# Weighting expert results on the way out of PSUM and adding them into memory with an accumulating scatter, in a decoder layer with a mixture of experts

## What is computed

```python
x = hidden_states.reshape(-1, 512)                       # 2048 tokens
topk_indices, topk_weights = router(x)                    # 2 of 16 experts for each token, weights sum to 1
combine = zeros(2048, 16).at[arange(2048)[:, None], topk_indices].add(topk_weights)
h1 = einsum('th,ehi->tei', x, w_up)                       # w_up (16, 512, 256)
a = relu(h1)**2 * combine[:, :, None]
routed = einsum('tei,eih->th', a, w_down)                 # w_down (16, 256, 512)
shared = relu(hidden_states @ shared_up)**2 @ shared_down
out = x_residual + routed + shared
```

## Time and profile before

| | |
|---|---|
| median of 3 runs | 1241.31 us (1241.05 to 1241.61) |
| profiled execution, its own time | 1238.74 us |
| its span in the trace | 1236.9 us |
| TensorE busy in the span | 1073.2 us (87%) |
| VectorE, ScalarE, GpSimd busy | 806.6, 668.3, 673.2 us |
| DMA | 94.74 MB, mean 77 GB/s |

### The profile page before, as it was taken

How to read it: one execution, slowest core, us unless ns; L and a number is a source line. 1 busy time by engine, 2 the same in 40 slices (tenths; PEclk the granted TensorE clock), 3 DMA queues, 4 the chain that set the end, 5 groups by cost and what they waited for, 6 DMA issues and landing times. The chain is left out here.

```text
span 1236.9 us, 18614 instructions
## 1 busy us (share of the span) xinstructions
PE 1073.2 (87%) x6368; PEld 642.0 (52%) x6368; DVE 806.6 (65%) x1195; ACT 668.3 (54%) x1438; POOL 673.2 (54%) x587
## 2 busy tenths in 40 slices
PE   7999838888888888888888899999999989999970
PEld 3444325555555555555555444444444457676740
DVE  5477779999999999999999476631760013333327
ACT  3566768889888888898888424202010012223220
POOL 1033369999999999999999630202041124444430
PEclk9999959999999999999999999999999999999995
DMA  6210001101111111111331212103027314333219
GB/s 204 87 36 19 18 18 35 35 28 35 35 36 32 30 35 36 36 33 63 95 102 45 90 48 103 69 34 116 20 79 244 102 44 128 127 128 129 77 49 385
DMA packets 51820, 94.74 MB, mean 77 GB/s; under 512 B 9806, under 2 KB 17998, under 8 KB 51728
## 3 DMA queue, kind: packets, MB, share of 16 engines
q1 hardware_dynamic: 44208, 72.82, 17.9%
q0 software_dynamic: 7520, 20.72, 5.4%
HBM read 74.51 MB, written 20.84 MB: 77 GB/s over the span
## 5 line engine op out<-in xcount | busy, mean ns | idle before, releaser
L604 POOL TENSOR_TENSOR w_all<-w_all 128x512 f32<-128x512 f32 x256 | 321.1, 1275 | 0.6 <-POOLq L96 0.3
L778 DVE TENSOR_TENSOR_SCAN w_all<-da,w_all 128x512 f32<-128x512 f32 x256 | 298.0, 1206 | 0.0
L712 ACT ACTIVATE da<-w_all,a_flat 128x512 f32<-128x512 f32 x256 | 179.6, 702 | 9.0 <-PEq L96 7.7
L683 PE MATMUL yb<-ident,w_all 128*128 128x128 f32 x1024 | 161.6, 281 | 7.5 <-DVE acc L786 7.5
L633 PE MATMUL sc<-w_all,attn 32*128 32x384 f32 (+3 forms) x512 | 105.0, 486 | 45.5 <-ACT w_all L720 22.8
L720 ACT ACTIVATE w_all<-sc,neg_max 128x128 f32<-128x128 f32 (+3 forms) x256 | 134.1, 539 | 16.5 <-DVE neg_max L770 15.5
L659 PE MATMUL ob<-w_all,v 128*32 128x128 f32 x1280 | 94.7, 277 | 52.8 <-ACT w_all L729 52.8
L683 PEld LDWEIGHTS yb<-ident,w_all 128*128 128x128 f32 x1024 | 113.5, 141 | 37.0 <-issue 30.6
L770 DVE TENSOR_REDUCE neg_max<-sc 128x2 f32<-128x256 f32 (+3 forms) x128 | 104.2, 814 | 34.2 <-PE sc L636 34.2
L1166 POOL TENSOR_TENSOR w_all<-w_all 128x512 f32<-128x512 f32 x24 | 29.4, 1226 | 165.0 <-ACT w_all L1337 165.0
L729 ACT ACTIVATE w_all<-tb 128x256 f32<-128x256 f32 (+2 forms) x192 | 102.8, 535 | 29.7 <-PE tb L648 29.7
(11 more groups left out here) (199 smaller groups left out, 1630.6 us busy)
## 6 DMA issues: line engine op xcount, KB each, us to landing
w_all<-b_scratch SPq DMA_DIRECT2D x64, 256.0 KB, 3.3
w_all<-in_w_up SPq DMA_DIRECT2D x16, 512.0 KB, 6.0
w_all<-in_w_down SPq DMA_DIRECT2D x16, 512.0 KB, 6.8
w_all<-sorted_y SPq DMA_DIRECT2D x16, 512.0 KB, 10.3
attn<-in_x SPq DMA_DIRECT2D x4, 1024.0 KB, 6.8
w_all<-in_x SPq DMA_DIRECT2D x16, 256.0 KB, 4.1
norms<-attn SPq DMA_DIRECT2D x4, 1024.0 KB, 4.3
out_dram<-acc SPq DMA_DIRECT2D x16, 256.0 KB, 8.9
```

What stands on the lines that cost most here:

```text
L604: pool.tensor_tensor(dbu[:, k, :], keep["du"][i // N][:, k * T:(k + 1) * T], b_all[i % 2][:, :], ALU.mult).then_inc(pool_dbu.sem, pool_dbu ...
L683: last = pe.transpose(yb[which][:, k * P:(k + 1) * P], state[i % 2][:, k, t * P:(t + 1) * P], ident[:, :])
L712: act.activation(da[unit % 2][:, :], keep["dt"][i // N][:, k * T:(k + 1) * T], ACT.Exp, scale=keep["a_flat"][:, unit % (N * KD):unit % (N ...
L778: dve.tensor_tensor_scan(state[i % 2][:, k, :], da[unit % 2][:, :], dbu[:, k, :], 0.0, ALU.mult, ALU.add).then_inc(dve_scan.sem, dve_scan. ...
```

## The change

The four things that it does:

1. The router also sorts the weights. Each weight, in float32, is cut into three bfloat16 parts (`high`, `mid`, `low`); three more planes are made from them, `collect` takes five planes at once (235 columns where 94 were), and `tokens` adds the three parts up to `slot_weight`, a weight for each slot.
2. ScalarE's copy of a tile's result out of PSUM multiplies by `slot_weight`.
3. The scatter adds: with `compute_op=ALU.add` it adds each row of `y` to the token's own row of `sorted_y`, in which `base` was stored before. A token has two pairs, in different tiles, so each scatter waits for the one before it to land. Padding is no longer dropped; it goes to 128 spare rows.
4. `acc` is stored to `sorted_y` in `close` (4 MB in 7 DMAs, `store_base`), and at the end 8 DMAs of 512 KB copy `sorted_y` to `out`, from memory to memory. The read back, the 32 instructions of VectorE and the 16 output DMAs are gone.

The scratch of the router moves with it (slot 15 of the weights is used, so expert 15 is loaded behind `s_routed`; `prob` and `tmp` lie in it).

```diff
 class Router:
...
-        self.prob = sb("prob", [P, TT, E])
+        self.prob = room[2][:, 0:TT * E].rearrange("p (t e) -> p t e", e=E)
...
-            last = pe.matmul(out[:, 0:2 * SLOT_TILES], self.in_row[:, n, :], self.planes[:, n, :, :].rearrange("p w i -> p (w i)"),
+            last = pe.matmul(out[:, 0:PLANES * SLOT_TILES], self.in_row[:, n, :], self.planes[:, n, :, :].rearrange("p w i -> p (w i)"),
                              start=(n == 0), stop=(n == 2 * B * NT - 1))
...
         for w, token in enumerate((self.token_hi, self.token_lo)):
             self.link(dve, dve.tensor_tensor(self.planes[:, :, w, :], self.in_tile[:, :, :], over(token[:, :], NI), ALU.mult))
+        weight = self.r["weight_all"][:, :]
+        high, mid, low = [x[:, :] for x in self.part_bf]
+        left, rest = [x[:, :] for x in self.part]
+        self.link(dve, dve.tensor_copy(high, weight))
+        self.link(dve, dve.tensor_tensor(left, weight, high, ALU.subtract))
+        self.link(dve, dve.tensor_copy(mid, left))
+        self.link(dve, dve.tensor_tensor(rest, left, mid, ALU.subtract))
+        self.link(dve, dve.tensor_copy(low, rest))
+        for w, part in enumerate((high, mid, low)):
+            self.link(dve, dve.tensor_tensor(self.planes[:, :, 2 + w, :], self.in_tile[:, :, :], over(part, NI), ALU.mult))
         dve.tensor_tensor(self.in_row, over(self.row[:, :], P), each(self.row_id[:, :], P), ALU.is_equal).then_inc(self.s_inverse, 1)
...
-        self.link(dve, dve.scalar_tensor_tensor(pair, token, 2.0, choice, ALU.mult, ALU.add))
-        self.link(dve, dve.tensor_scalar(none, token, 0.0, float(4 * B * T), ALU.is_lt, ALU.mult))
+        self.link(dve, dve.tensor_scalar(none, token, 0.0, self.spare_row[:, 0:1], ALU.is_lt, ALU.mult))
+        self.link(dve, dve.tensor_copy(slot_weight, high))
+        self.link(dve, dve.tensor_tensor(slot_weight, slot_weight, mid, ALU.add))
+        self.link(dve, dve.tensor_tensor(slot_weight, slot_weight, low, ALU.add))
...
 def close(nc, d, keep, r):
...
-            sp.wait_ge(pool_xb.sem, pool_xb.upto(4 * LAST + 3))
-            expert(15)
...
+            def store_base(b):
+                sp.wait_ge(dve_base.sem, dve_base.upto(4 * b + 3))
+                sp.dma_start(d["sorted_y"][b * T:(b + 1) * T, :].rearrange("(t p) c -> p t c", p=P),
+                             keep["acc"][:, b, :].rearrange("p (t c) -> p t c", c=D)).then_inc(r["s_base"][b], 16)
+
+            store_base(0)
...
-            for e in (0, 1, 7, 13):
+            for e in (0, 1, 7, 13, 15):
                 expert(e)
...
+            store_base(1)
+            store_base(2)
             sp.wait_ge(pe_up.sem, pe_up.upto(FK * B - 1))
             for e in (14, 2, 3):
                 expert(e)
+            for t in four:
+                sp.wait_ge(dve_base.sem, dve_base.upto(4 * LAST + t))
+                sp.dma_start(d["sorted_y"][LAST * T + t * P:LAST * T + (t + 1) * P, :], keep["acc"][:, LAST, t * D:(t + 1) * D]).then_inc(r["s_base"][LAST], 16)
...
 def tiles(nc, d, keep, ctx, r):
...
-        for t in range(TT):
-            sp.dma_start(back[t], d["sorted_y"][2 * t * P:2 * (t + 1) * P, :].rearrange("(p k) c -> p (k c)", k=2)).then_inc(s_g[t], 16)
-        with sp.Fori(0, B) as b:
-            for t in range(NT):
-                pair.wait(sp, b * NT + t, "second")
-                sp.dma_start(d["out"][b, t * P:(t + 1) * P, :], keep["acc"][:, b, t * D:(t + 1) * D]).then_inc(s_o, 16)
-        sp.wait_ge(s_o, 16 * TT)
+        for t in range(TT // 2):
+            b, h = t // 2, t % 2
+            sp.dma_start(d["out"][b, h * 2 * P:(h + 1) * 2 * P, :].rearrange("(p k) c -> p (k c)", k=2),
+                         d["sorted_y"][t * 2 * P:(t + 1) * 2 * P, :].rearrange("(p k) c -> p (k c)", k=2)).then_inc(s_o, 16)
+        sp.wait_ge(s_o, 16 * (TT // 2))
...
         def store(i):
             act_l.wait(pool, i, "y")
-            pool.indirect_dma_start(out=d["sorted_y"][0:2 * B * T, :], in_=y[i % 2], in_offset=None, bounds_check=2 * B * T - 1, oob_is_err=False,
-                                    out_offset=bass.IndirectOffsetOnAxis(ap=r["pair_i"][:, i:i + 1], axis=0))\
+            if i == 0:
+                for b in range(B):
+                    pool.wait_ge(r["s_base"][b], 16 * (NT if b == B - 1 else 1))
+            else:
+                pool.wait_ge(s_y[(i - 1) % 2], 16 * ((i - 1) // 2 + 1))
+            pool.indirect_dma_start(out=d["sorted_y"][0:B * T + P, :], in_=y[i % 2], in_offset=None, compute_op=ALU.add,
+                                    out_offset=bass.IndirectOffsetOnAxis(ap=r["row_i"][:, i:i + 1], axis=0))\
                 .then_inc(s_y[i % 2], 16)
...
-                act_l.done(act.activation(y[s1], bank[6 + s1][:, :], ACT.Copy), "y")
+                act_l.done(act.activation(y[s1], bank[6 + s1][:, :], ACT.Copy, scale=r["slot_weight"][:, i - 1:i]), "y")
...
-        for t in range(TT):
-            dve.wait_ge(s_g[t], 16)
-            acc = keep["acc"][:, t // NT, (t % NT) * D:(t % NT + 1) * D]
-            for k in range(2):
-                if k == 1:
-                    pair.wait(dve, t, "first")
-                pair.done(dve.scalar_tensor_tensor(acc, back[t][:, k * D:(k + 1) * D], r["weight"][k][:, t:t + 1], acc, ALU.mult, ALU.add),
-                          ("first", "second")[k])
```

More of the change, by code:

```diff
@@ L806, in _ @@
                     normalize(spread_in(g))
-CONSTANTS = 12
+CONSTANTS = 13
+PLANES = 5
 class Router:
@@ L823, in __init__ @@
         self.bias = sb("bias", [P, E])
-        self.prob = sb("prob", [P, TT, E])
+        self.prob = room[2][:, 0:TT * E].rearrange("p (t e) -> p t e", e=E)
         self.hot = [sb(f"hot{k}", [P, TT, E]) for k in range(2)]
         self.scratch = room[1][:, 0:3 * TT * E]
-        self.tmp = sb("tmp", [P, TT, E])
+        self.tmp = room[2][:, TT * E:2 * TT * E].rearrange("p (t e) -> p t e", e=E)
         g = room[0][:, 2 * TT * (SLOT_TILES + 1):]
@@ L853, in __init__ @@
         self.in_row = room[2].bitcast(BF16).rearrange("p (n q) -> p n q", q=P)
-        self.planes = room[3].bitcast(BF16)[:, 0:PAIRS * 2 * SLOT_TILES].rearrange("p (n w i) -> p n w i", n=PAIRS, w=2)
+        self.planes = room[3].bitcast(BF16)[:, 0:PAIRS * PLANES * SLOT_TILES].rearrange("p (n w i) -> p n w i", n=PAIRS, w=PLANES)
+        self.part_bf = [sb(f"part_bf{n}", [P, PAIRS], BF16) for n in range(3)]
+        self.part = [sb(f"part{n}", [P, PAIRS]) for n in range(2)]
+        self.spare_row = sb("spare_row", [P, 1])
         self.index = [room[0][:, n * SLOT_TILES:(n + 1) * SLOT_TILES] for n in range(4)]
@@ L877, in constants @@
                 (self.row_id, [[1, P]], 0, 0), (self.tile_row, [[P, SLOT_TILES + 1]], 0, 0),
-                (self.token_hi, [[0, 2], [1, B * NT]], 1, 0), (self.token_lo, [[P, 2], [0, B * NT]], 0, 1)):
+                (self.token_hi, [[0, 2], [1, B * NT]], 1, 0), (self.token_lo, [[P, 2], [0, B * NT]], 0, 1), (self.spare_row, [[0, 1]], B * T + P, 1)):
             pool.iota(out[:, :], pattern, base=first, channel_multiplier=per_partition,
@@ L1040, in tokens @@
         dve.wait_ge(self.s_token, 1)
-        hi, lo = psum[:, 0:SLOT_TILES], psum[:, SLOT_TILES:2 * SLOT_TILES]
+        hi, lo, high, mid, low = [psum[:, w * SLOT_TILES:(w + 1) * SLOT_TILES] for w in range(PLANES)]
         choice, token, pair, none = self.index
+        slot_weight = self.r["slot_weight"][:, :]
         self.link(dve, dve.tensor_scalar(choice, lo, float(P), None, ALU.is_ge))
@@ L1046, in tokens @@
         self.link(dve, dve.tensor_tensor(token, token, pair, ALU.add))
-        self.link(dve, dve.scalar_tensor_tensor(pair, token, 2.0, choice, ALU.mult, ALU.add))
-        self.link(dve, dve.tensor_scalar(none, token, 0.0, float(4 * B * T), ALU.is_lt, ALU.mult))
+        self.link(dve, dve.tensor_scalar(none, token, 0.0, self.spare_row[:, 0:1], ALU.is_lt, ALU.mult))
+        self.link(dve, dve.tensor_copy(slot_weight, high))
+        self.link(dve, dve.tensor_tensor(slot_weight, slot_weight, mid, ALU.add))
+        self.link(dve, dve.tensor_tensor(slot_weight, slot_weight, low, ALU.add))
         self.link(dve, dve.tensor_scalar(self.r["token_i"][:, :], token, 0.0, None, ALU.max))
-        dve.tensor_tensor(self.r["pair_i"][:, :], pair, none, ALU.add).then_inc(self.r["s_routed"], 1)
+        dve.tensor_tensor(self.r["row_i"][:, :], token, none, ALU.add).then_inc(self.r["s_routed"], 1)
 def close(nc, d, keep, r):
@@ L1086, in close @@
         bank = [ctx.enter_context(nc.psum_tensor(f"pc{i}", [P, 512], F32)) for i in range(8)]
-        router = Router(nc, ctx, keep, r, [r["w_all"][:, e, :] for e in (7, 13, 0, 1)])
+        router = Router(nc, ctx, keep, r, [r["w_all"][:, 7, :], r["w_all"][:, 13, :], r["w_all"][:, 15, :], keep["arena"][:, 0:2 * SLOT]])
         four, eight = range(4), range(FK)
@@ L1492, in experts @@
             "w_all": keep["w_all"],
-            "weight": [sb(f"weight{k}", [P, B * NT])[:, :] for k in range(2)],
```

(10 more changed lines are left out.)

## The result

The change makes the kernel slower: 1308.93 us median of 4 runs (1305.68 to 1313.04), 1241.18 before in the same comparison, ratio 1.055 (95% interval 1.052 to 1.059). The forecast was 1249.4 with a range to 1292; the time lies outside it. The profiled execution took 1310.16 us, its span is 1307.6, 70.7 more than in the earlier trace rows.

What follows compares the result with a forecast made beforehand. TensorE was taken to bound the tile loop and DMA time the tail. Router 7.4 + columns 1.9 + clock 1.9 + block's end 0.5 + loop 12.7 - tail 16.3 = +8.1, so 1249.4 us; own range 1242 to 1290, whole range 1233 to 1292.

Steps and rivals of the forecast that it cites:

- the period: Tile loop: time per tile, the larger of TensorE's 4.10 us and landing plus release; forecast 4.3, loop +12.7.
- L: Tile loop: time from an adding scatter's start on POOL to its landing, taken as 4.0 us.
- the gap: Tile loop: time from one scatter's landing to the next one's start on POOL, taken as 0.3 us like a gather's.
- The formula quoted from the Trainium skill: Scatter: about 2.0 us fixed plus bytes over 436 GB/s, giving 3.2 us and a hidden wait.
- slow adder: Rival, tile loop: adding at half rate, landing 5.3 us, period 5.6, loop +73.8, total 1310.5; chance 0.18.
- Router: Router's end: eight new VectorE instructions ahead of collect make TensorE wait 7.4 us, bounds 6.4 and 8.5.
- the five short instructions: Router's end: five new VectorE instructions on 32 elements, 1.1 us together.
- The columns: Router's end, TensorE: collect's 32 matmuls grow from 94 to 235 columns, +1.9 us, bounds 1.5 and 2.3.
- the clock: Router's end: TensorE restarts at clock 0.50 after the new wait, +1.9 us, bounds 0 and 4.7.
- The block's end: Before the tile loop: SP's last store of acc stands before the barrier, +0.5 us, bounds 0 and 1.
- Tail: After the last landing: a 4.19 MB memory copy, 14.9 us between 9.9 and 19.9, tail 17.8, gain 16.3.
- Hidden wait: Rival, tile loop: L at most 3.8 keeps the period 4.10; 1239.2 us, 1234.2 with the fastest copy; chance 0.37.

Runs made afterwards that it cites:

- e3: Changed kernel with the scatter's two waits swapped, so the DMA instruction itself holds the wait for the landing; 1286.04 us, ratio 1.036.
- e5: Changed kernel with padding given an index past the bound and dropped by the scatter again; 1286.03 us, ratio 1.036.
- e6: Changed kernel, but the adding scatter takes only the first 256 of a row's 512 columns; 1262.54 us, from one execution.
- e4: Changed kernel with collect put behind down(2) instead of ahead of it; 1300.16 us, ratio 1.049.
- e1: Changed kernel with every wait kept, but the scatter writes instead of adding; 1235.46 us, ratio 0.9965.
- e7: Changed kernel with even and odd tiles adding to two arrays, no wait between scatters, padding dropped, collect behind down(2), an adding copy at the end; 1237.97 us, ratio 0.9969.
- e2: Changed kernel, still adding, but each slot has its own row and no scatter waits for the one before; 1236.86 us, ratio 0.9972.
- e8: The two-array version with SP, not POOL, waiting for the last adding DMAs; 1237.23 us, ratio 0.9976.

## Why the prediction was wrong

- **The step that failed** is the sentence "I take 4.0, between the ends, at the sum of reads in turn", with "I take 0.3, as the new call has no bounds check". The mechanism was the one forecast: the scatters in series set the loop. Both terms of the period were too small. L was 4.8 for 4.0, the gap about 0.8 for 0.3, the period 5.63 for 4.3. 46 x 1.33 is 61 of the 62 us by which the loop missed; some 38 of them are L's and 23 the gap's; e3 gave 23 us back.
- **Inside L** the forecast had 2.1 for an empty scatter, 0.6 for its bytes, 0.6 for the read of memory and 0.6 for the second stream. Measured: 2.1, then 0.6 for longer building (e5), then 2.0 for all bytes (e6). The building was named as possible growth and left out of the value, and that was the larger error; the bytes were near, 2.0 for 1.8. The rate at which a DMA adds could not be read from the trace of before. The formula quoted from the Trainium skill ("DMA: Bandwidth & Descriptors", "Anatomy of one DMA — SWDGE (gpsimd) path") gave 3.2; the trace doesn't agree, with 4.8.
- **The gap** had its row: 0.8 of the old scatter. I put it down to the bounds check's MOVE and took the gather's 0.3. What decides is which instruction holds the wait (e3): 0.3 is right for a DMA that holds it itself, 0.8 for one that stands behind it. Before, the MOVE held ScalarE's wait; in the changed kernel a wait instruction holds the landing's, and without any bounds check the gap is the same. With the bounds check back it is 0.85 (e5, 1114.65 to 1115.50), so the check itself is worth less than 0.1. The nearer row was the scatter's own.
- **The forecast of the slow adder** had +73.8 for the loop, by L = 5.3 and a gap of 0.3; the loop measured +74.4, by 4.8 and 0.8. The number was right by two errors that cancel: the adder is not slow enough for it.
- **The range** ended at L = 4.9, which holds the measured L, but always with the gap of 0.3: its other bound of 0.8, worked out in the text, was not carried into the range. With it the range would have reached 46 x 5.7 + 4.9 = 267.1, +78 in the loop, 1315. The chance of 0.14 for all times above 1292 is also too small by the text's own numbers: the slow adder alone, at 1310.5, had 0.18.
- **Router**: right, +10.8 for 11.2; a wait of 7.49 for 7.4, the five short instructions 1.8 (the first took 0.90) for 1.1 and the three long ones 5.97 for 6.3. The columns cost 1.9 as forecast (e4), the clock 1.3 for 1.9, and up to 2.5 in other executions. The block's end: nothing seen, -0.6 for +0.5.
- **Tail**: -18.1 for -16.3; the copy moved its bytes in about 13 us, at 98 to 459 GB/s by stretches of 1 us, nearer to once-counted bytes (9.9) than to twice (19.9). Right in mechanism.
- **Hidden wait**: this rival would have needed L + gap of at most 4.1; e1 shows what it gives, 1235.5 (forecast 1239.2, and 1234.2 with a fast copy).

## What to carry to other kernels

A wait that puts DMAs in series has a period of landing plus release gap, and both must be priced from the row of the very instruction that will stand there; an error in either is multiplied by the number of links (here 46). Before serialising adding scatters, see whether two targets break the series: in e7, from the first scatter to the last landing, the loop took 189.6 us where the changed kernel took 263.5, 74 less, for 13 more at the end. And when a DMA of POOL has several waits, let the DMA itself hold the one that is met last (e3, 23 us).

## What the runs showed of the hardware

- An adding scatter of 128 rows of 2 KB took 1.59 us of building on POOL (0.99 when it writes, e1) and 4.8 to landing (2.7), of which 2.0 go with the bytes (0.6).
- The gathers that POOL issues between the scatters landed in 4.2 to 4.4 us beside adding scatters (changed kernel) and in 3.4 beside writing ones (e1). In e2, where they took 4.2 to 4.3, the loop kept TensorE's pace all the same.
- A memory to memory add ran at 197 to 234 GB/s with all DMA engines busy (e7), a memory to memory copy at 320 GB/s on average and up to 459.
- A POOL DMA that follows a separate wait starts some 0.5 us later than one that holds the wait itself (e3).
- When the last DMAs are POOL's, 5 to 6.6 us passed between the last bytes and the end of the span, whoever waited (e7, e8); with SP's copies it was under 2 (changed kernel: last bytes at 1305.8, end at 1307.6).
- VectorE's products of 1504 elements took either 1.73 or 2.45. In the changed kernel the five take 1.73, 2.45, then 1.73, 2.45, 1.73. The trace shows what goes with it: each one of 2.45 began while a product of GpSimd over 512 elements was running (911.92 within 910.35 to 912.78, 917.98 within 917.21 to 918.84), each one of 1.73 while GpSimd did nothing. The first short instruction, 0.90 where the next of its kind take 0.18, began within such a product too (914.40 within 913.78 to 915.26). The products of GpSimd took 1.04 when they met none of these, and 1.5 to 2.4 otherwise. No run was made to separate the two.
